# A selective scan between two expert layers: the decay factors move from PSUM to an SBUF ring, and the C rows get a second PSUM pair

## The reference

```python
x = x + 0.5 * ffn(layernorm(x))
x = x + mamba(layernorm(x))
x = x + 0.5 * ffn(layernorm(x))
```

```python
dA = jnp.exp(dt_t[..., None] * A)                       # A = -exp(A_log)
h = dA * h + (dt_t * x_t)[..., None] * B_t[:, None, :]
y_t = jnp.einsum('bds,bs->bd', h, C_t)
...
y = ys + xc * D_skip
y = y * silu(z)
out = layernorm(y @ W_out) * ln_g + ln_b
```

## Time and profile before

| | |
|---|---|
| median of 3 runs | 528.58 us (523.49 to 529.66) |
| profiled execution, its own time | 530.37 us |
| its span, first to last instruction | 528.6 us |
| mean granted TensorE clock | 0.862 |
| recurrence, first `inject` to the end of the last scan | 183.34 to 391.17 us |
| after it: gate, projection, norm, second expert layer | 391.17 us to the end |

### The profile page before, as it was taken

How to read it: one execution, slowest core, us unless ns; L and a number is a source line. 1 busy time by engine, 2 the same in 40 slices (tenths; PEclk the granted TensorE clock), 3 DMA queues, 4 the chain that set the end, 5 groups by cost and what they waited for, 6 DMA issues and landing times. The chain is left out here.

```text
span 528.6 us, 6538 instructions
## 1 busy us (share of the span) xinstructions
PE 376.4 (71%) x1914; PEld 257.2 (49%) x1915; DVE 381.3 (72%) x532; ACT 190.4 (36%) x309; POOL 318.0 (60%) x214
## 2 busy tenths in 40 slices
PE   4549999919964247667776877677775366999990
PEld 4549999916321112223323523222233355899990
DVE  4563545447979899988999799989975956454533
ACT  2303443316698133422333333323412340334430
POOL 2024777526015299998999889989950202577750
PEclk8668999968995569969898999899989575999996
DMA  7941111130006057667556656675405220111115
GB/s 237 354 113 31 50 45 47 37 90 1 0 11 208 0 198 245 200 224 240 201 206 206 232 175 207 218 232 198 161 0 225 93 81 16 31 45 49 46 34 169
DMA packets 35604, 68.09 MB, mean 129 GB/s; under 512 B 5633, under 2 KB 20546, under 8 KB 35586
## 3 DMA queue, kind: packets, MB, share of 16 engines
q1 hardware_dynamic: 32642, 61.84, 35.8%
q0 software_dynamic: 2944, 6.04, 4.1%
HBM read 61.44 MB, written 6.42 MB: 128 GB/s over the span
## 5 line engine op out<-in xcount | busy, mean ns | idle before, releaser
L715 POOL TENSOR_TENSOR phase<-dtx,w_sb 128x1024 f32<-128x1024 f32 x64 | 151.3, 2394 | 19.6 <-DVE dtx L963 9.5
L745 DVE TENSOR_TENSOR_SCAN phase<-psum,phase 128x1024 f32<-128x1024 f32 x64 | 144.7, 2280 | 6.3 <-POOL phase L715 6.0
L791 ACT ACTIVATE psum<-dt,neg_A 128x1024 f32<-128x1024 f32 x64 | 71.4, 1118 | 138.5 <-DVE phase L745 126.5
L338 POOL DMA_INDIRECT phase<-xn_rows,gather_row x46 | 46.1, 1002 | 86.6 <-DMA xn_rows<-xn_tok 30.6
L557 PE MATMUL psum<-phase 128*128 128x128 f32 x736 | 94.4, 284 | 1.4 <-ACT phase L492 1.4
L557 PEld LDWEIGHTS psum<-phase 128*128 128x128 f32 x736 | 89.9, 199 | 3.0 <-ACT phase L492 2.8
L825 PE MATMUL psum<-phase,ident 128*128 128x512 f32 x176 | 86.5, 615 | 0.0
L818 PE MATMUL psum<-bc_parts,pick_row 128*128 128x512 bf16 x88 | 28.9, 413 | 71.8 <-DVE phase L755 54.5
L449 DVE TENSOR_TENSOR phase<-phase,psum 128x512 f32<-128x512 f32 x46 | 31.6, 688 | 59.5 <-PE psum L557 59.5
L344 POOL DMA_INDIRECT y_rows<-phase,scatter_row x46 | 48.5, 1054 | 23.7 <-ACT phase L499 21.2
L818 PEld LDWEIGHTS psum<-bc_parts,pick_row 128*128 128x128 bf16 x88 | 6.1, 100 | 108.2 <-DVE phase L755 84.8
(11 more groups left out here) (149 smaller groups left out, 387.8 us busy)
## 6 DMA issues: line engine op xcount, KB each, us to landing
w_sb<-bc_rows SPq DMA_DIRECT2D x84, 512.0 KB, 4.5
w_sb<-ffn_w SPq DMA_DIRECT2D x16, 512.0 KB, 8.2
w_sb<-ffn_w SPq DMA_DIRECT2D x8, 256.0 KB, 8.0
xn_rows<-xn_tok SPq DMA_DIRECT2D x8, 256.0 KB, 3.5
xnT<-y_rows SPq DMA_DIRECT2D x8, 256.0 KB, 3.8
out<-x_tok SPq DMA_DIRECT2D x4, 256.0 KB, 2.4
phase<-xn_rows,gather_row POOLq DMA_INDIRECT x46, 2.6
y_rows<-phase,scatter_row POOLq DMA_INDIRECT x46, 2.3
```

The lines of the kernel that those rows point to most:

```text
L338: nc.gpsimd.indirect_dma_start(xs_sb[:, t % 2, :], None, xn_rows, bass.IndirectOffsetOnAxis(ap=gather_row[:, t:t + 1], axis=0)).then_inc(f ...
L715: nc.gpsimd.tensor_tensor(dBx[:, k % X_RING, :], dtx[:, h, batch[b]], B_sb[:, k % B_RING, :], ALU.mult).then_inc(M["dBx_ready"], 1)
L745: nc.vector.tensor_tensor_scan(H[:, k % H_RING, :], dA_bank[k % 2], dBx[:, k % X_RING, :], 0.0, ALU.mult, ALU.add).then_inc(M["scan_done"], 1)
L791: nc.scalar.activation(dA_bank[k % 2], dt[:, h, batch[b]], ACT.Exp, scale=neg_A[:, h * S + s:h * S + s + 1]).then_inc(M["dA_ready"], 1)
```

## The change

The decay factors go to a new ring of two SBUF tiles, `dA`, cut from `phase` between `H` and `dBx`. `phase` has room for the 12 tiles of 1024 (12288 of 12300 columns). PSUM banks 0 to 3, which held them, now hold two copies of the C row, used in turn; banks 4 and 5 are unused in the recurrence. `spread` of unit n then waits for product n - 2 in place of n - 1, two of them run ahead of the loop, and inside the loop the one for n + 2 stands right after the wait for product n, behind GpSimd's `add` and ahead of VectorE's.

```diff
-        H_RING, X_RING, HC_RING = 4, 3, 3
+        H_RING, X_RING, HC_RING, DA_RING = 4, 3, 3, 2
...
-        H, dBx, hC = carve((P, H_RING, L), (P, X_RING, L), (P, HC_RING, L))
+        H, dA, dBx, hC = carve((P, H_RING, L), (P, DA_RING, L), (P, X_RING, L), (P, HC_RING, L))
...
-        dA_bank = [two_banks(0), two_banks(2)]
-        C_bank = two_banks(4)
+        C_bank = [two_banks(0), two_banks(2)]
         y_bank = two_banks(6)
...
-                nc.vector.tensor_tensor_scan(H[:, k % H_RING, :], dA_bank[k % 2], dBx[:, k % X_RING, :], 0.0,
+                nc.vector.tensor_tensor_scan(H[:, k % H_RING, :], dA[:, k % DA_RING, :], dBx[:, k % X_RING, :], 0.0,
                                              ALU.mult, ALU.add).then_inc(M["scan_done"], 1)
...
-                nc.vector.tensor_tensor(hC[:, n % HC_RING, :], H[:, k % H_RING, :], C_bank, ALU.mult
+                nc.vector.tensor_tensor(hC[:, n % HC_RING, :], H[:, k % H_RING, :], C_bank[n % 2], ALU.mult
                                         ).then_inc(M["hC_ready"], 1)
...
-                if k >= 2:
-                    act.wait_ge(M["scan_done"], k - 1)
-                nc.scalar.activation(dA_bank[k % 2], dt[:, h, batch[b]], ACT.Exp,
+                if k >= DA_RING:
+                    act.wait_ge(M["scan_done"], k - DA_RING + 1)
+                nc.scalar.activation(dA[:, k % DA_RING, :], dt[:, h, batch[b]], ACT.Exp,
                                      scale=neg_A[:, h * S + s:h * S + s + 1]).then_inc(M["dA_ready"], 1)
...
-                if dve_index[k] >= 1:
-                    pe.wait_ge(M["hC_ready"], dve_index[k])
+                n = dve_index[k]
+                if n >= 2:
+                    pe.wait_ge(M["hC_ready"], n - 1)
                 for q in range(CPB):
-                    mm = nc.tensor.matmul(psum[:, 4 + q, :], pick_row[:, S + s:S + s + 1].broadcast_to([P, P]),
+                    mm = nc.tensor.matmul(psum[:, 2 * (n % 2) + q, :], pick_row[:, S + s:S + s + 1].broadcast_to([P, P]),
...
             spread(dve_units[0])
+            spread(dve_units[1])
...
-                if n is not None and n + 1 < len(dve_units):
-                    spread(dve_units[n + 1])
                 if s >= X_RING and k - X_RING in pool_index:
...
                 if n is not None:
                     pe.wait_ge(M["hC_ready"], n + 1)
+                    if n + 2 < len(dve_units):
+                        spread(dve_units[n + 2])
                     add(hC[:, n % HC_RING, :], M["summed"], s == S - 1)
```

## The result

The changed kernel takes **645.63 us** (median of 4 runs, 643.85 to 647.03) against 526.24 us before (4 runs): ratio 1.2263, 95% interval 1.2166 to 1.2361. The forecast was 646 us. The profiled execution took 644.6 us, with a span of 642.8 us.

A forecast was written before the change was run, and what follows sets the result against it. VectorE and GpSimd, both nearly full side by side, were taken to bound the recurrence. Turns add 117.0 us to the profiled 530.37, giving 647.4; the median 1.8 lower gives 645.6, forecast 646 us, range 628 to 672.

The forecast's parts named there:

- the main step: In the recurrence, scans with two SBUF operands and GpSimd's operations exclude each other, so their sum sets the pace: +117.0 us.
- The size: Recurrence from first inject to last scan's end: 324.8 us in place of 207.8, so +117.0 us.
- One GpSimd operation for each scan: In the recurrence, one GpSimd operation is released by each scan: 64 x 2.21 = 141.4 us.
- No idle time: In the recurrence, neither VectorE nor GpSimd leaves the pair idle; GpSimd's 20 extra products take its lead away: no idle time counted.
- The tail at 0: From last scan to last gate, 6.4 to 11.4 us against 9.22 before: -2.8 to +2.2 us, taken as 0.
- The untouched parts at 0: What follows the tail, norm and experts, is not touched by the change: no time counted.
- ScalarE: Its writes of decay factors to SBUF, 1.12 us per unit, are hidden by the scans: nothing; at most 72 us without cover.
- the C pair: Second C copy in the recurrence can shorten VectorE's waits (5.4 and 6.5 us), but VectorE is not the limit: nothing.
- access overhead: VectorE's scan reading SBUF instead of PSUM: the skill's rule gives about 4 us lower; the rows show no gain: nothing kept.
- The first (no exclusion): Rival: scans do not exclude GpSimd in the recurrence, C pair's gain counts, 11.7 us off, 517 us; chance 8%.
- The second (shared bandwidth: Rival: VectorE and GpSimd share bandwidth in the recurrence, not turns; 68 us on top of 198.5, about 587 us; chance 6%.
- The third (a gap at each hand-over): Rival: turns in the recurrence with costly hand-overs or idle turns, at full length or with waits between: 667 to 685 us; chance 12%.

The follow-up runs named there:

- The ring alone: Changed kernel with only the decay factors moved to SBUF; one C pair and TensorE's old order stay as before: 649.92 us, ratio 1.2299.
- the operand alone: Changed kernel, but the scan reads its first operand from PSUM banks 4 and 5, filled once; ScalarE still writes SBUF: 518.40 us, ratio 0.9792.
- GpSimd without reads: Changed kernel with each of GpSimd's 84 products in the recurrence replaced by two memsets, which write SBUF and read none: 509.09 us, one run.
- half of the scans: Changed kernel with even units' decay factors in PSUM, odd units' in SBUF, so 32 of 64 scans have two SBUF operands: 591.97 us, ratio 1.0947.
- the first four experiments: The ring alone, the operand alone, GpSimd without reads, and the changed kernel with all 64 C products on VectorE: 649.92, 518.40, 509.09, 612.02 us.

## Why the prediction was right

**What bounds it, and the main step: right, and shown.** The ring alone gives the loss, the operand alone takes it away, GpSimd without reads takes it away, and half of the scans give 42% of it.

**The size: 121.2 us in the recurrence for 117.0 forecast.** The ends of the 148 instructions (64 scans, 84 of GpSimd), each set against the end before it, give the terms:

| ended after | forecast | measured |
|---|---|---|
| scan after GpSimd | 64 x 2.13 = 136.3 | 58 x 2.15, together 124.6 |
| GpSimd after a scan | 64 x 2.21 = 141.4 | 57, together 127.2 |
| GpSimd after GpSimd | 20 x 2.35 = 47.1 | 26 x 2.34 = 60.7, and the first, 2.4 |
| scan after a scan | none | 6, together 14.2 |
| first inject to last scan's end | 324.8 | 329.0 |

The hand-overs read from five collisions in the stage before were right to 0.02 us. "One GpSimd operation for each scan" was a little off: six scans and six more GpSimd operations than forecast followed their own kind, and the first inject follows nothing. Two sources make up nearly all of the 4 us: 8 of the 57 turns were started by a semaphore (2.54 us in place of 2.19, 2.8 us together), and the last scan ended 3.31 us after the one before it in place of 2.18. GpSimd had finished by then, and VectorE's own product lay between them:

```profile
507.06 1.19 DVE L754 TENSOR_TENSOR phase<-phase,psum 128x1024 f32<-128x1024 f32 x1
508.17 2.28 DVE L744 TENSOR_TENSOR_SCAN phase<-phase 128x1024 f32<-128x1024 f32 x1
```

**No idle time: nearly.** Those are the idle moments of the pair, about 4 us. GpSimd's 20 extra products did not take its lead away everywhere: the eight semaphore turns are two runs of four with GpSimd three units ahead, each right after a scan of 9.1 us (see the last section).

**The tail at 0: -2.1 us.** The last gate began 7.1 us after the last scan, within the 6.4 to 11.4 worked out.

**The untouched parts at 0: -4.8 us, in part a difference from run to run.** The first inject came at 181.42 in place of 183.34 us. From the start of the last gate the rest took 125.3 us in place of 128.2. The traces of the first four experiments, whose code is the same in both places, scatter too: 179.2 to 184.0 us for the first and 125.9 to 127.5 for the second. Whether the change has a part in the 2.9 us of the second no run shows. TensorE's clock bears on it: the first 16 matmuls of the first tile in the second expert layer took 3.79 us before and 2.05 us after. Before, at a granted clock of 0.50, the lower of its two levels (1.2 GHz; 446 to 450 us):

```profile
446.73 3.79 PE L557 MATMUL psum<-phase 128*128 128x128 f32 x16 [0.36 <-ACT phase L492]
```

After, at 1.00, the upper one (2.4 GHz; 563 to 566 us):

```profile
563.30 2.05 PE L557 MATMUL psum<-phase 128*128 128x128 f32 x16 [0.35 <-ACT phase L492]
```

So 121.2 - 2.1 - 4.8 = 114.3 us, to rounding the difference of the spans (642.8 - 528.6). The forecast met the median to 0.4 us by luck: errors of 4.2 and -6.9 us cancel to -2.7, and the last 2.8 us come from the step to the median, taken as 1.8 us below the profiled execution, while the changed kernel's median lies 1.0 us above its own. The accuracy of the forecast is that of the terms, some 1%.

**ScalarE, the C pair, access overhead.** Right at nothing, and each shown: 1149 ns hidden under 239.7 us of waits; the pair at 10.4 us where VectorE is the bound and nothing where it is not. The shortest scan from SBUF is 2258 ns, from PSUM 2260, and with no GpSimd reads all 64 from SBUF have a median of 2285 ns, against 2283 with the first operand in the fixed PSUM bank. The Trainium skill's smaller access overhead for VectorE on SBUF (Perfetto Trace Analysis, "Optimizing Scalar/DVE Operations") is not seen when one operand of a scan moves; the other operand and the output were in SBUF in both.

**The rivals.** The first (no exclusion) fell with every stretched scan. The second (shared bandwidth, 587 us) fell with the single turns: 58 scans end 2.14 to 2.15 us after a GpSimd operation's end, so that the loser had done at most 0.15 us of its 2.26 to 2.29 until then. The third (a gap at each hand-over) fell with the same 2.15 us; of its waits between turns only the 4 us above were there. The 115 ns that the forecast took from the Trainium skill (SBUF — State Buffer, "A bandwidth-pool intuition that's wrong") are measured there on a DMA whose descriptors GpSimd writes, not on two engines' instructions, and no hand-over to a dispatched instruction shows such a gap here.

## What to carry to other kernels

Before moving an operand of a VectorE instruction from PSUM to SBUF, count its tile operands in SBUF, and look whether GpSimd reads SBUF at that time. Two of them beside a busy GpSimd meant turns here, for the scan as for tensor_tensor, and what costs time is then the sum of the two engines, not the larger. In such a place work with one operand in PSUM is free on VectorE, so that moving work from GpSimd to VectorE can make the kernel faster although VectorE looks the busier of the two (646 to 612 us here). Look for a collision elsewhere in the trace: a duration of 3.18 us beside one of 1.23 us for the same instruction gave the price of the whole change.

## What the runs showed beside that

Turns are not always fair. A scan that is dispatched within about 0.1 us after the start of a GpSimd operation was passed over for up to two more of them. GpSimd in the changed kernel, three in a row and then the fourth:

```profile
301.47 9.10 POOL L714 TENSOR_TENSOR phase<-dtx,w_sb 128x1024 f32<-128x1024 f32 x3
310.55 2.33 POOL L724 TENSOR_TENSOR w_sb<-phase,w_sb 128x1024 f32<-128x1024 f32 x1
```

The scan meanwhile:

```profile
305.88 9.14 DVE L744 TENSOR_TENSOR_SCAN phase<-phase 128x1024 f32<-128x1024 f32 x1 [1.11 <-POOL phase L714]
```

It ends at 315.02, 2.14 us after the fourth GpSimd operation (312.88). This happened at 7 of the 12 scans dispatched so close; the other five got the next turn. One more scan, dispatched 0.65 us into a GpSimd operation after an inner gate, was passed over for one. What decides is open. It costs little, because the pair is in use all the same and GpSimd then comes to the end of its ring: five times two scans followed each other, and twice GpSimd's next four turns waited for a semaphore, 2.8 us in all.
